# The last block of a chained feed-forward kernel: weight checks with two buffers loaded from ScalarE's queue, and the last output tile reloaded into another buffer

## The reference

```python
decay = exp(-exp(w)) * (0.5 + 0.5 * tf)          # tf = sigmoid(sum(cond))
# forward and backward scans over the 1024 tokens of
#   a = a * decay + exp(k) * v ;  b = b * decay + exp(k)
mixed = sigmoid(r) * num / max(den, 1e-8) * (0.8 + 0.2 * tf)
h = einsum('bsd,fd->bsf', mixed, W1)             # 1024 -> 4096
q = clip(round(h / 0.1), -32768, 32767)
a = gelu(q * 0.1)
out = x + einsum('bsf,df->bsd', a, W2)           # 4096 -> 1024
```

## Time and profile before

| | us |
|---|---|
| median of 3 runs | 1729.12 |
| profiled execution | 1728.37 |
| its span | 1726.6 |
| TensorE busy in the span | 1648.9 (96%) |
| VectorE busy | 1232.5 (71%) |
| ScalarE busy | 986.4 (57%) |
| block 7 begins on TensorE at | 1508.9 |
| last output product ends on TensorE at | 1711.4 |

### The profile page before, as it was taken

The page is one execution under the profiler, slowest core; times in us unless marked ns, Lnnn a source line. Parts: engine busy times, 40 slices in busy tenths (PEclk is TensorE's granted clock), DMA queues, the critical chain, the costliest instruction groups (busy, mean ns, idle before and its releaser), DMA issues. The chain is left out here.

```text
span 1726.6 us, 30636 instructions
## 1 busy us (share of the span) xinstructions
PE 1648.9 (96%) x12258; PEld 1199.1 (69%) x12258; DVE 1232.5 (71%) x1684; ACT 986.4 (57%) x1558; POOL 139.2 (8%) x155
## 2 busy tenths in 40 slices
PE   1699999999999999999999999999999999999996
PEld 0234445888578884888658885688847887488863
DVE  8888797878768658687677767786886875854131
ACT  4577423765666565674747656476666647465341
POOL 0000110011000101002010010001010010100101
PEclk9799999999999999999999999999999999999998
DMA  8979895688575866769386684868757694676754
GB/s 237 237 183 275 276 333 172 218 254 220 127 244 188 252 177 183 237 200 262 122 218 236 214 232 127 235 215 248 226 137 217 204 247 151 175 243 200 195 185 98
DMA packets 131205, 362.54 MB, mean 210 GB/s; under 512 B 14000, under 2 KB 28592, under 8 KB 130096
## 3 DMA queue, kind: packets, MB, share of 16 engines
q1 hardware_dynamic: 105216, 308.33, 52.8%
q0 software_dynamic: 25840, 52.18, 17.8%
HBM read 333.19 MB, written 81.79 MB: 240 GB/s over the span
## 5 line engine op out<-in xcount | busy, mean ns | idle before, releaser
L813 PE MATMUL ps<-mo,w_ring 128*128 128x256 f16 x6272 | 695.1, 273 | 5.1 <-DVE q L1758 2.7
L813 PEld LDWEIGHTS ps<-mo,w_ring 128*128 128x128 f16 x6272 | 613.1, 98 | 82.5 <-issue 7.1
L957 PE MATMUL ps<-act,w_ring 128*128 128x512 f16 x1760 | 383.3, 379 | 0.0
L876 PE MATMUL ps<-act,w_ring 128*128 128x256 f16 x3136 | 348.1, 273 | 0.7
L876 PEld LDWEIGHTS ps<-act,w_ring 128*128 128x128 f16 x3136 | 305.8, 98 | 38.4 <-issue 2.5
L957 PEld LDWEIGHTS ps<-act,w_ring 128*128 128x128 f16 x1760 | 172.2, 98 | 203.2
L1784 DVE SCALAR_TENSOR_TENSOR act<-a,act 128x1024 f16<-128x1024 f32 x72 | 87.8, 1222 | 91.3 <-ACT act L1233 91.3
L1223 ACT ACTIVATE a<-q 128x1024 f32<-128x1024 int16 x124 | 131.0, 1057 | 7.0 <-DVE act L1784 2.0
L724 POOL DMA_DIRECT2D out_dram<-xy x56 | 66.9, 1195 | 810.6 <-ACT xy L1257 709.6
L1746 DVE SCALAR_TENSOR_TENSOR ps<-sp,ps 128x512 f32<-128x512 f32 x70 | 48.4, 692 | 110.2 <-issue 49.4
L754 PE MATMUL ps<-mo,w_ring 128*128 128x512 f16 x256 | 66.7, 424 | 56.8 <-DMA w_ring<-w_half 34.9
(11 more groups left out here) (132 smaller groups left out, 1812.0 us busy)
## 6 DMA issues: line engine op xcount, KB each, us to landing
w_ring<-w1s SPq DMA_DIRECT2D x168, 512.0 KB, 5.7
w_ring<-w_half SPq DMA_DIRECT2D x130, 512.0 KB, 5.5
w_ring<-w2s SPq DMA_DIRECT2D x56, 512.0 KB, 5.1
out_dram<-xy POOLq DMA_DIRECT2D x111, 256.0 KB, 6.2
tt<-in_w_dram SPq DMA_DIRECT2D x48, 512.0 KB, 5.3
V<-in_fside_dram SPq DMA_DIRECT2D x64, 256.0 KB, 5.6
R<-in_x_dram SPq DMA_DIRECT2D x64, 256.0 KB, 5.9
w_half<-in_w_dram POOLq DMA_DIRECT2D x16, 1024.0 KB, 10.3
```

Of the source, the lines that this page charges most:

```text
L813: mm = pe.matmul(dst[:, f, :], wp_ring[:, k, r, f, q, :], mo[:, op, q, p, :], start=(fresh and f == 0 and q == 0 and p == 0), stop=(q == K ...
L876: mm = pe.matmul(dst[:, i, :], wy_ring[:, k, i, 2 * s + j, :], ao[:, s, op, j, p, :], start=(fresh and i == 0 and s == 0 and j == 0 and p ...
L957: mm = pe.matmul(bank[d][:, :], w2_ring[:, k, FPS * (s - SPLIT) + j, :], act[:, act_at(n, s) + j, p, :], start=(s == SPLIT and j == 0 and ...
```

## The change

The change touches the last block alone. (1) The reload of the last output tile goes into the first quarter of `a32`, the Gelu's buffer. It no longer waits for the add of output tile 5; it waits for the low part of the last activation (`s_alo`), which is the last reader of `a32`. (2) Checks 48 to 63 have two float32 buffers and two int8 buffers, used in turn. Their loads are issued from ScalarE's queue (`end_load`), and SP's queue has none of them. (3) The checks stand in other places: two in each of the steps `s` = 2, 3, 4, one in each of the next six places, then 60 and 61 before output 0, 62 before output 1, 63 before output 2; the outputs 2 to 6 follow one another.

```diff
-        end_full = m_st[:, 0, :, :].rearrange("p k t -> p (k t)")
-        end_i8 = m_st[:, 2, 0, 0:T // 2].bitcast(I8)
+        end_full = [m_st[:, k, :, :].rearrange("p k t -> p (k t)") for k in range(2)]
+        end_i8 = [m_st[:, 2, 0, k * T // 2:(k + 1) * T // 2].bitcast(I8) for k in range(2)]
...
                 for k in range(4):
                     sp.wait_ge(s_acc[k], 16 * added(n, 8))
-                sp.wait_ge(s_acc[1], 16 * (added(n, 2 * DT - 3) + 1))
-                sp.dma_start(x_in[:, 1, :], out[n // 2, 1 - n % 2, d]).then_inc(s_x[1], 16)
+                sp.wait_ge(s_alo, lo_half(n, LAST, 1) + 1)
+                sp.dma_start(a32[:, 0, :], out[n // 2, 1 - n % 2, d]).then_inc(s_x[1], 16)
...
             def check_i8(at):
                 full, small = check_buffers(at)
-                act_e.wait_ge(s_chkload, 16 * (at + 1))
+                act_e.wait_ge(s_chkload[at % 2], 16 * (at // 2 + 1))
                 if at < END_CHECKS:
                     act_e.wait_ge(s_gelu, half_of(at // DT + 1, SPLIT - 1 if at % DT < 2 else LAST, 1) + 1)
-                if at > 0:
-                    act_e.wait_ge(s_chk, at)
+                    if at > 0:
+                        act_e.wait_ge(s_chk, at)
+                elif at >= END_CHECKS + 2:
+                    act_e.wait_ge(s_chk, at - 1)
                 sc.activation(small, full, ACT.Copy, scale=W_SCALE).then_inc(s_chki8, 1)
+
+            def end_load(at):
+
+                act_e.wait_ge(s_chk, at - 1)
+                if at == END_CHECKS:
+                    act_e.wait_ge(s_mo, 3 * KH * (BLOCKS - 1))
+                act_e.dma_start(check_buffers(at)[0], check_rows(at)).then_inc(s_chkload[at % 2], 16)
+
+            def end_check_i8(*ats):
+
+                for at in ats:
+                    if END_CHECKS < at < 2 * STEPS * FPS - 1:
+                        end_load(at + 1)
+                    check_i8(at)
...
                 quads_hi_11(n, 0)
+                if not nxt:
+                    end_load(at)
+                    end_load(at + 1)
                 for s in range(2, SPLIT + 1):
...
                     if not nxt:
-                        check_i8(at + s - 2)
+                        end_check_i8(at + 2 * s - 4, at + 2 * s - 3)
...
-                    check_i8(at + 15)
-                    output_out(n, 4, 5, 6)
+                    end_check_i8(at + 12, at + 13)
+                    output_out(n, 0)
+                    end_check_i8(at + 14)
+                    output_out(n, 1)
+                    end_check_i8(at + 15)
+                    output_out(n, 2, 3, 4, 5, 6)
```

More of the change, by code:

```diff
@@ L252, in adaln_ffn_kernel @@
         s_store = [sem(f"s_store{k}") for k in range(2)]
-        s_chkload = sem("s_chkload")
+        s_chkload = [sem(f"s_chkload{k}") for k in range(2)]
         s_chki8 = sem("s_chki8")
@@ L648, in ffn_block @@
                     load_tile(g0 + CT)
[L649 to L653 removed]
+                if nxt:
+                    load_check(at + 5)
+                ring_load(2)
                 if nxt:
@@ L1966, in chained_block @@
                     if not nxt:
-                        check(at + s - 2)
+                        check(at + 2 * s - 4)
+                        check(at + 2 * s - 3)
                     seed_u4(hid(n, s))
@@ L1982, in chained_block @@
                 mix(2, 2)
-                check(at if nxt else at + 3)
+                check(at if nxt else at + 6)
                 mix(2, 3)
@@ L1986, in chained_block @@
                 mix(3, 0, 1)
-                check(at + 1 if nxt else at + 4)
+                check(at + 1 if nxt else at + 7)
                 seed_u4(part_y(n, 1))
@@ L1997, in chained_block @@
                 if not nxt:
-                    check(at + 5)
+                    check(at + 8)
                 mix(4, 3)
@@ L2006, in chained_block @@
                 if not nxt:
-                    check(at + 6)
+                    check(at + 9)
                 quantise22(n, SPLIT + 2)
@@ L2011, in chained_block @@
                 if not nxt:
-                    check(at + 7)
+                    check(at + 10)
                 seed_u4(hid(n, LAST))
@@ L2017, in chained_block @@
                 if not nxt:
-                    check(at + 8)
+                    check(at + 11)
                 act_lo(n, SPLIT + 2, 1)
@@ L2023, in chained_block @@
                 act_lo(n, LAST, 1)
[L2024 to L2027 removed]
+                if not nxt:
+                    for k in range(12, 16):
+                        check(at + k)
+                    return
+                convert(n + 1, 0)
                 mix(6, 1)
[L2029 removed]
+                check(at + 2)
                 mix(6, 2)
[L2031 to L2032 removed]
                 mix(6, 3)
                 mix(7, 0)
[L2035 to L2038 removed]
+                convert(n + 1, 1)
                 mix(7, 1)
[L2040 removed]
+                check(at + 3)
                 mix(7, 2, 3)
[L2042 to L2050 removed]
+                check(at + 4)
+                divide(g0 + 7)
+                convert(n + 1, 2)
+                convert(n + 1, 3)
+                check(at + 5)
                 if n + 2 < BLOCKS:
```

121 lines of the change are left out of this document (38 added, 83 removed).

## The result

The kernel after takes 1719.8 us, the median of five runs (1718.73 to 1722.27), against 1728.91 us for the kernel before in the same set. The profiled execution took 1719.94 us, of which 1718.2 are the span.

What follows compares the result with a forecast made beforehand. TensorE was taken to bound the kernel up to its last product's end, 1711.41, with 15.19 us following. A gain of 8.85 and a loss of 3.1 gave -5.75 us, so 1723.4 us from the median; range 1720.9 to 1727.0.

Steps and rivals of the forecast that it cites:

- The end: After TensorE's last product: reload no longer late, 6.34 us follow in place of 15.19, a gain of 8.85 us.
- SP's queue and step 2: Last block: sixteen load issues leaving SP gain zero; the check pair in step 2 just fits, zero loss.
- Step 3: Last block, checks 50 and 51: load issued about 1550.3, lands after 4.2 us, TensorE waits 1.5 us.
- Step 4: Last block, checks 52 and 53: load lands after 4.8 us, low parts late, TensorE 2.9 us late in all.
- The place of the earlier trace: Conversion 55, ahead of a `seed_u4` TensorE already waited for: a load issue ahead of it costs 0.2 us.
- Loss: TensorE's delay in the last block: 2.9 + 0.2 = 3.1 us, bounds 1.1 and 7.5 us.
- the quick one: Rival: loads in the pairs land in 3.8 us twice, issued under a running instruction; loss 1.1, 1721.4 us; chance 0.12.
- The dear issue: Rival: a load issue on ScalarE takes 1.2 us; loss 5.9, 1726.2 us; chance 0.09.
- The slower rival: Rival: waits in the pairs make TensorE's clock fall twice; loss 14.1, 5.3 us slower, 1734.4 us; chance 0.04.

Runs made afterwards that it cites:

- loads-early kernel: Kernel after with the loads of checks 51 and 53 issued behind `spill_p5` of steps 3 and 4; 1718.88 us, ratio 0.9949; run again 1719.14 us, 0.9951.

## Why the prediction missed

**The end: right.** -8.85 predicted, -8.96 measured, by the mechanism given: reload at 1674.91 (about 1676 predicted), second sum directly behind TensorE, output 6's add hidden. The prediction credited the change's two parts together; the runs show that the checks' part brings all of it and that the reload alone brought 2.1 us.

**SP's queue and step 2: right.** Both zero. The first conversion there ended 0.88 us ahead of the time in the earlier trace rows, with block 7 itself 0.86 earlier, and `seed_u4` was done 0.93 us ahead of the 1543.8 that the prediction worked out.

**Step 3: the delay right, 1.41 us against 1.5, by luck: two errors nearly cancel.** (The predicted 1.5 is counted from 1556.10, the start without a wait, so it stands against 1.41 and not against the listed 1.24.) "ScalarE issues its load only when it comes to the pair, at about 1550.3" was wrong. Set on before's time (block 7 began 0.86 earlier after), the load went out at 1549.41, 0.9 us sooner, because the sequencer had run past the instructions that the engine still had before it. The rows of before had the moment in them: its Gelu (L1223) ends at 1548.23 + 1.06 = 1549.29, and 0.10 us behind that is 1549.39. The landing was 4.99 us and not 4.2, which took 0.8 of it back.

**Step 4: the term that failed.** It was to bring the delay from 1.5 to 2.9 us, through the low parts of group 3. It brought nothing: the product behind them was as late as TensorE had been since step 3. The same early issue put the load at 1562.17, on before's time 1563.03 in place of 1563.9, and it landed in 3.84 us and not 4.8. So the sums started 1.9 us sooner than in my working: 1568.85 is 1569.71 on before's time, against 1571.6. The second short product would then be 2.9 - 1.9 = 1.0 us late, less than the 1.41 TensorE had lost already. In the trace the first of its two low parts ends at 1573.18 + 2.35 / 2 = 1574.4, and the product starts eight matmuls after 1574.11, at 1575.0. The rule that I had taken for a landing, "nearer to the median of 5.2", was the wrong choice here; the landings that count were 4.99 and 3.84, one over and one under my value.

**The place of the earlier trace rows: zero, not 0.2.** The load issue is at 1609.25, in the same moment as the output copy that stands ahead of it in the program:

```profile
1609.25 0.60 ACT L1241 ACTIVATE xy<-ps 128x512 f32<-128x512 f32 x1 [6.39 <-PE ps L860]
1609.25 0.35 ACTq L1266 DMA_DIRECT2D m_st<-in_w_dram  x1
...
1612.78 1.22 PEld L860 LDWEIGHTS ps<-act,w_ring 128*128 128x128 f16 x12 [0.36 <-issue]
```

The gap before the weights is 0.36 us as before. The issue runs under the copy.

**Loss: 1.42 us in place of 3.1.** It is the delay of step 3, the listed wait of 1.24 and the 0.17 us of overlap that a wait takes away. Of the rivals, the quick one has the nearest price, 1.1 us, but half of its ground: an issue that overlaps, in step 4 the landing of 3.8, in step 3 not. The dear issue didn't happen. The longest issue, 1.42 us, was the second of two back to back at 1525.8, next to two of SP's, where nothing waits:

```profile
1525.76 1.42 ACTq L1266 DMA_DIRECT2D m_st<-in_w_dram  x1
```

In the pairs an issue took 0.33 us. The Trainium skill's rule that such a record can hold a wait for the shared descriptor generator ("Perfetto Trace Analysis", DMA Instruction — HWDGE) would fit the 1.42; it changes no term.

**The range: too narrow below for a reason that was in none of its terms.** The forecast was 1723.4, the measured median 1719.8, 3.6 us less. Half of it, 1.8 us, is the terms above: block and tail changed by -7.54 and not by -5.75, which with before's 1729.12 would give 1721.6, inside the range. The other 1.8 us are in no term. In the profiles only the part ahead of block 7 moves by so much from one execution to the next, and the three sets gave differences of 9.1, 5.7 and 8.5 us. The prediction bounded its unknown costs carefully and gave the rest of the program, where starts differ by 7.5 us from one execution to another, no width at all.

**The slower rival's mechanism is real, and nearer than the 0.04 it was given suggests.** It took one wait ahead of each of the two loads, which sends them out 3.3 us later. Then they land late too, TensorE waits 5 to 8.5 us twice, the clock falls each time, and the kernel takes 1738 to 1739 us, 10 to 14 us more than before in the same set. The price of a fall was 2.9 us by the earlier trace rows; here the two falls cost 4.7 us in one kernel and 217.60 - 203.91 - (11.4 - 1.24) = 3.5 in the other. In block 7, 5.15 us is the shortest wait around which it fell; after 1.24 us the clock stood at 1.00:

```profile
1556.00:1560.00 4.00, 3.36 (x31) 3.04 (x32) 3.93 (x6) 3.97 (x6) 0.00 (x0) 1.00 0.91 354
```

So long a wait isn't needed, and the length of the wait doesn't decide it alone. Early in the span, behind a wait of 2.18 us that ended at 95.26, the loads-early kernel's second execution had 0.50; in its first, behind a wait of 3.01 us that ended at 95.06, the clock stayed at 1.00. These are the stretches of 2 us, that of the shorter wait first:

```profile
96.00:98.00 2.00, 2.00 (x6) 0.69 (x5) 1.86 (x4) 1.97 (x5) 0.00 (x0) 0.50 1.23 262
...
96.00:98.00 2.00, 2.00 (x11) 0.92 (x10) 1.86 (x4) 1.94 (x5) 0.00 (x0) 1.00 0.61 131
```

What else decides it, no run here separates.

## What to carry to other kernels

Put a load into the order of the engine that uses it at the place where its buffer comes free, not at the place where it is used; count its issue from the last wait ahead of it on that engine, not from the engine's last instruction. When two changes go in together, ask which one already contains the other's gain. And before giving a range of a few microseconds on a span of 1700, find out how much the untouched part of the program scatters, and read the effect from the touched block, cut at two moments of the trace.

## What the runs showed of the hardware

- ScalarE's sequencer issued a DMA up to 0.84 us before the engine started an instruction that stands ahead of it in program order, and moving the load by one activation moved the issue by 0.08 us. It went out 0.10 us behind the Gelu for which an instruction ahead of it waits.
- An issue of a 512 KB load from ScalarE took 0.33 to 0.44 us, and 1.42 beside two of SP's; it cost the engine nothing where an activation was running.
- The granted clock fell to 0.50 around TensorE waits of 6.20 to 8.48 us in block 7, stood at 0.67 in the stretch behind one of 5.15, and was 0.50 behind one of 2.18 us early in the span; it was 1.00 behind waits of 1.24 and 3.01 us.
- 512 KB on ScalarE's queue landed after 3.84 and 4.99 us with the next load over 3 us behind, 6.70 and 7.39 with one directly behind it, and 8.69 to 9.81 counted from the issue of one directly ahead. A second queue didn't make landings shorter: the sixteen check loads had a median of 5.8 us and a longest of 9.2 in the kernel after, against 5.2 and 6.6 before, with their issues at other moments. That agrees with the Trainium skill ("DMA: Bandwidth & Descriptors", Issuing engines are not separate DMA queues): DMAs from all issuing engines run on the same 16 DMA engines.
